# Gathers issued before scatters in each pass of an expert-choice feed-forward layer, on one Trainium2 core

## What is computed

```
def ffn(x, gate_w, w_gate, w_up, w_down):
    affinity = softmax(einsum('bsd,ed->bse', x, gate_w)).transpose(0, 2, 1)
    gating, idx = top_k(affinity, 256)              # each of 8 experts takes 256 of 1024 tokens
    x_in = x[bidx, idx]                             # gather
    h = silu(x_in @ w_gate[e].T) * (x_in @ w_up[e].T)
    x_e = h @ w_down[e].T
    return zeros_like(x).at[bidx, idx].add(gating[..., None] * x_e)   # scatter with add

x = x + 0.5 * ffn(layernorm(x), ...)
x = x + attention(layernorm(x), ...)                # 16 heads of 8, rotary in three dimensions
x = x + 0.5 * ffn(layernorm(x), ...)
```

## Time and profile before

| | us |
|---|---|
| three runs | 1326.4, 1331.73, 1332.17 (median 1331.73) |
| profiled execution, its own time | 1333.52 |
| its span, first to last instruction | 1331.7 |
| PE busy | 1122.5 (84%) |
| DVE busy | 1044.5 (78%) |
| ACT busy | 768.2 (58%) |
| POOL busy | 448.9 (34%) |

### The profile page before, as it was taken

The page is one execution under the profiler, slowest core; times in us unless marked ns, Lnnn a source line. Parts: engine busy times, 40 slices in busy tenths (PEclk is TensorE's granted clock), DMA queues, the critical chain, the costliest instruction groups (busy, mean ns, idle before and its releaser), DMA issues.

```text
span 1331.7 us, 25142 instructions
## 1 busy us (share of the span) xinstructions
PE 1122.5 (84%) x9424; PEld 476.4 (36%) x9424; DVE 1044.5 (78%) x2182; ACT 768.2 (58%) x1433; POOL 448.9 (34%) x431
## 2 busy tenths in 40 slices
PE   3159898999487999999899998899978889889884
PEld 3126565666131222222222222122313256556553
DVE  3676966764986999999999999899896685975531
ACT  2043112532246999999789996889778843121120
POOL 3034777688256111100000000004000025777674
PEclk9999999999587999999999998999999988999887
DMA  8023446456612311112201131101220224444442
GB/s 264 6 56 68 82 86 141 82 128 139 174 43 80 87 31 38 43 43 52 63 17 31 41 82 48 40 8 41 73 57 4 56 58 95 100 87 85 104 89 20
DMA packets 92122, 94.54 MB, mean 71 GB/s; under 512 B 14464, under 2 KB 68992, under 8 KB 91968
## 3 DMA queue, kind: packets, MB, share of 16 engines
q1 hardware_dynamic: 69472, 76.13, 20.5%
q0 software_dynamic: 22528, 16.79, 9.6%
HBM read 63.12 MB, written 31.59 MB: 71 GB/s over the span
## 4 chain that ended last, share of the span: by engine, by line
DVE 50%; PE 25%; POOL 8%; issue 7%; ACT 5%; DMA 3%; DVEq 0%; POOLq 0%; ACTq 0%
DVE mx L1549 34%; PE pA L1072 4%; PE pS L1061 4%; DVE ge L1275 4%; POOL out_dram L553 3%; PE pO L1185 3%; PE pO L1062 2%; DMA xg<-zd,idx 2%; DVE onehot L1362 2%; POOL x L553 2%; ACT Pt L893 2%; DVE scr L1434 2%; PE pS L1206 2%; POOL xg L535 2%; PE pS L1062 1%
## 5 line engine op out<-in xcount | busy, mean ns | idle before, releaser
L1549 DVE TENSOR_REDUCE mx<-pA 128x2 f32<-128x1024 f32 x512 | 589.3, 1216 | 26.8 <-PE pA L1117 25.3
L893 ACT ACTIVATE Pt<-pS 128x512 f32<-128x512 f32 x1024 | 556.2, 596 | 75.7 <-PE pS L1206 70.3
L1185 PE MATMUL pO<-Pt,Vst 128*16 128x256 f32 x4096 | 327.9, 393 | 11.5 <-ACT U L884 11.5
L793 ACT ACTIVATE Pt<-pS 128x512 f32<-128x512 f32 x128 | 76.3, 597 | 245.6 <-PE pS L1061 245.4
L595 POOL TENSOR_TENSOR mparts<-mx,onesm 128x32 bf16<-128x32 f32 x16 | 4.0, 252 | 518.0 <-DVE mx L1554 511.3
L1117 PE MATMUL pA<-Kst,Qst 48*128 48x512 bf16 x704 | 144.3, 406 | 36.6 <-DVE mx L1549 34.8
L535 POOL DMA_INDIRECT xg<-zd,idx x128 | 125.7, 982 | 142.0 <-issue 73.1
L1061 PE MATMUL pS<-Pt,wg 128*128 128x512 f32 x256 | 147.6, 660 | 14.5 <-DVE Pt L1394 9.4
L1206 PE MATMUL pS<-Qst,Kst 51*128 51x512 bf16 x704 | 141.5, 398 | 10.7 <-ACT Pt L893 5.1
L1185 PEld LDWEIGHTS pO<-Pt,Vst 128*16 128x16 f32 x4096 | 68.3, 94 | 206.5 <-issue 116.7
L1072 PEld LDWEIGHTS pA<-wd,Pt 128*128 128x128 f32 x1024 | 120.9, 192 | 20.3 <-issue 15.0
(11 more groups left out here) (170 smaller groups left out, 1140.0 us busy)
## 6 DMA issues: line engine op xcount, KB each, us to landing
wg<-w_gate_dram SPq DMA_DIRECT2D x32, 256.0 KB, 2.8
wu<-w_up_dram SPq DMA_DIRECT2D x32, 256.0 KB, 3.1
wd<-w_down_dram SPq DMA_DIRECT2D x32, 256.0 KB, 3.9
qk<-parts SPq DMA_DIRECT2D x64, 96.0 KB, 2.7
Kst<-qk SPq DMA_DIRECT2D x132, 32.0 KB
zd<-Z SPq DMA_DIRECT2D x8, 512.0 KB, 4.1
vp<-pair SPq DMA_DIRECT2D x4, 1024.0 KB, 5.3
Vst<-vp SPq DMA_DIRECT2D x16, 256.0 KB
```

Source lines behind the costliest of these rows:

```text
L893: S.activation(Pt[:, s % 4, j, r * 512:(r + 1) * 512], pS[:, bank_of(k, 4 * s + 2 * j + r), :], ACT.Exp, scale=SCALE).then_inc(s_exp, 1)
L1185: last = M.matmul(pO[32 * h:32 * h + 16, cols], Vst[k][:, s % 8, h, :], Pt[:, s % 4, h // 2, (h % 2) * 512 + 256 * a:(h % 2) * 512 + 256 * ...
L1549: V.reduce_max(mx2[:, k, 2 * j:2 * j + 2, c, half], pA[ring[q, a] % 2][:, :, :], AX.X).then_inc(s_Ar, 1)
```

## The change

Three things change; all sums stay the same apart from the order in which three parts of a factor are added.

1. POOL's order in a pass: `gather(it + 2)` stands ahead of `scatter(it - 1)`, in both FFNs, except in pass 22.
2. The `rest` and `lowest` of parts 0 and 1 move from POOL to DVE (passes 12 to 14); those of parts 2 and 3 stay on POOL, after `scatter(15)`. `middle(2)` on ACT moves from pass 15 to behind it. On SP, `load(0)` and `load(1)` move ahead of `load_weights(16)`, and `store_parts(2)` behind the reload of X.
3. `expert_values`, which copied one expert's slots and factors, is gone; `onehots` and `compact` read them in place. `pick` reads PSUM in place with two reductions, where it copied to `picked` and added three times. Its waits and the four buffers of `idx` stay.

```diff
             for it in range(RUN):
-                if 13 <= it:
-                    lowest(it - 13)
-                if it in (12, 13):
-                    rest(it - 12)
+                if it + 2 < RUN:
+                    gather(it + 2)
                 if it:
                     scatter(it - 1)
-                if it + 2 < RUN:
-                    gather(it + 2)
                 if it == 2:
                     gains(1)
-                if it in (14, 15):
-                    rest(it - 12)
             scatter(RUN - 1)
+            rest(2)
+            rest(3)
+            lowest(2)
             lowest(3)
...
             for it in range(RUN, NIT):
+
+                if it + 2 < NIT and it != 22:
+                    gather(it + 2)
                 if it > RUN:
                     scatter(it - 1)
-                if it + 2 < NIT:
+                if it == 22:
                     gather(it + 2)
...
-            def expert_values(j):
-                hh = j // E
-                dve.wait_ge(s_vals, 6 * (hh + 1))
-                V.tensor_copy(slotE[:, :], slotT[hh % 2][:, :, j % E])
-                link(V.tensor_copy(valsE[:, :, :], vals[hh % 2][:, :, j % E, :]))
...
-                    last = V.tensor_scalar(onehot[:, b, c, :], slots[:, :], slotE[:, c * HB + b:c * HB + b + 1], None, ALU.is_equal)
+                    last = V.tensor_scalar(onehot[:, b, c, :], slots[:, :], slotT[j // E % 2][:, c * HB + b, e:e + 1], None,
+                                           ALU.is_equal)
...
-                link(V.tensor_copy(picked[r][:, :, :], pI[:, 0:5 * HB * SH].rearrange("p (k f) -> p k f", f=5)))
-                V.tensor_tensor(idx[r][:, :], picked[r][:, :, 0], picked[r][:, :, 1], ALU.add).then_inc(s_idx, 1)
+                picked = pI[:, 0:5 * HB * SH].rearrange("p (k f) -> p k f", f=5)
+                V.reduce_sum(gain[r][:, :], picked[:, :, 2:5], AX.X)
+                V.reduce_sum(row[:, :], picked[:, :, 0:2], AX.X).then_inc(s_row, 1)
+                dve.wait_ge(s_row, j + 1)
+                V.tensor_copy(idx[r][:, :], row[:, :]).then_inc(s_idx, 1)
...
-                link(V.tensor_tensor(gsum[:, :], picked[r][:, :, 2], picked[r][:, :, 3], ALU.add))
-                link(V.tensor_tensor(gain[r][:, :], gsum[:, :], picked[r][:, :, 4], ALU.add))
...
+                if (it, k) == (12, 1):
+                    rest(0)
+                if (it, k) == (12, 3):
+                    lowest(0)
+                if (it, k) == (13, 2):
+                    rest(1)
+                if (it, k) == (14, 0):
+                    lowest(1)
```

More of the change, by code:

```diff
@@ L160, in program @@
         res = [sb(f"res{i}", [P, CH, ROWS_H], F32) for i in range(2)]
-        slotE = sb("slotE", [P, HT], F32)
-        valsE = sb("valsE", [P, HT, 5], BF16)
         onehot = sb("onehot", [P, HB, CH, CAP], BF16)
-        picked = [sb(f"picked{i}", [P, HB * SH, 5], F32) for i in range(4)]
-        gsum = sb("gsum", [P, HB * SH], F32)
+        row = sb("row", [P, HB * SH], F32)
         idx = [sb(f"idx{i}", [P, HB * SH], I32) for i in range(4)]
@@ L247, in program @@
         s_comp = sem("comp")
+        s_row = sem("row")
         s_idx = sem("idx")
@@ L468, in _ @@
             store_parts(1)
+            load(0)
+            load(1)
+            store_values(1)
             load_weights(16)
-            load(0)
             load_weights(17)
-            store_parts(2)
-            store_values(1)
             for b in range(2, B):
@@ L476, in _ @@
                 load_x(b, x1_in)
+            store_parts(2)
             store_parts(3)
-            load(1)
             store_values(2)
@@ L770, in between @@
                     middle(1)
-                if (it, k) == (15, 0):
-                    middle(2)
                 if (it, k) == (16, 1):
@@ L815, in _ @@
                 expert(it)
+            middle(2)
             middle(3)
@@ L1036, in compact @@
                     pe.wait_ge(s_idx, j)
+                if j % E == 0:
+                    pe.wait_ge(s_vals, 6 * (j // E + 1))
                 for b in range(HB):
@@ L1371, in pick @@
                         dve.wait_ge(s_scat[b], adds_before(j - 4) + 32)
-                link(V.tensor_copy(picked[r][:, :, :], pI[:, 0:5 * HB * SH].rearrange("p (k f) -> p k f", f=5)))
-                V.tensor_tensor(idx[r][:, :], picked[r][:, :, 0], picked[r][:, :, 1], ALU.add).then_inc(s_idx, 1)
+                picked = pI[:, 0:5 * HB * SH].rearrange("p (k f) -> p k f", f=5)
[3 more added lines that the diff above has]
+                V.tensor_copy(idx[r][:, :], row[:, :]).then_inc(s_idx, 1)
                 if j >= NIT - E:
-                    V.scalar_tensor_tensor(idxo[r][:, :], picked[r][:, :, 0], float(HB * N), picked[r][:, :, 1], ALU.add, ALU.add)
-                link(V.tensor_tensor(gsum[:, :], picked[r][:, :, 2], picked[r][:, :, 3], ALU.add))
-                link(V.tensor_tensor(gain[r][:, :], gsum[:, :], picked[r][:, :, 4], ALU.add))
+                    V.tensor_scalar(idxo[r][:, :], row[:, :], float(HB * N), None, ALU.add)
             def outputs(j):
@@ L1420, in setup, with rest, lowest @@
                     add_products(u)
+            def rest(u):
+                dve.wait_ge(s_hi, u + 1)
+                V.tensor_tensor(scr[:, 2 + u % 2, :], scr[:, u % 2, :], parts[:, u % 2, 0, :], ALU.subtract).then_inc(s_rest, 1)
+            def lowest(u):
+                dve.wait_ge(s_mid, u + 1)
+                V.tensor_tensor(parts[:, u % 2, 2, :], scr[:, 2 + u % 2, :], parts[:, u % 2, 1, :], ALU.subtract).then_inc(s_parts, 1)
             def add_products(u):
@@ L1485, in expert @@
                 if not first and it + 2 < end and it + 2 not in (8, 24):
-                    onehots(3)
+                    onehots(it + 2, 3)
                 hidden(it, 1)
@@ L1493, in expert @@
                     if quarters:
-                        expert_values(it + 3)
-                        onehots(0)
+                        onehots(it + 3, 0)
                 between(it, 2)
@@ L1500, in expert @@
                 if quarters and it != 22:
-                    onehots(1)
+                    onehots(it + 3, 1)
                 between(it, 3)
@@ L1507, in expert @@
                     pick(24)
-                    expert_values(25)
-                    onehots(0)
-                    onehots(1)
+                    onehots(25, 0)
+                    onehots(25, 1)
                 if quarters:
-                    onehots(2)
+                    onehots(it + 3, 2)
                 between(it, 4)
             def all_onehots(j):
-                expert_values(j)
                 for quarter in range(4):
-                    onehots(quarter)
+                    onehots(j, quarter)
             def first_experts(j):
```

6 lines of the change are left out of this document (3 added, 3 removed).

## The result

The changed kernel took 1364.62 us (median of 4 runs, 1363.81 to 1365.63) beside 1330.16 us for the kernel before on the same chip (median of 4 runs, 1326.4 to 1332.17): ratio 1.0263, 95% interval 1.0236 to 1.0290. It is **slower** by 2.6%. The forecast was 1332.3 us in a range of 1316 to 1347, so the result lies 17.6 us above the range. The profiled run took 1365.63 us, its span is 1363.8 us, 32.1 us above the span before.

A forecast was written before the change was run, and what follows sets the result against it. It took PE's 24.5 us of waits for gathers queued behind scatters as the bound in plain passes. First FFN +1.3 and second -0.7 gave +0.6 us on a median of 1331.7: 1332.3 us, range 1316 to 1347.

The forecast's parts named there:

- -2.3: First FFN: with `rest` off POOL's passes, the last `pick` step is no longer slowed (2.20 us instead of 0.17): -2.3 us.
- Issue to landing 3.4 us: Plain passes: time from a scatter's issue to its landing, which `pick` waits for, taken as 3.4 us.
- the loop of 15.5 us: Plain passes: gather issues, scatter issues, landing, `pick`, next gather form a closed loop, 15.5 us a pass against 14.1 before.
- The bounds: Loop period: 15.0 us with minimum issues and a 3.2 us landing, 16.5 us with gathers near their longest.
- one with norms and projections its own 15.9: First FFN, experts 6 to 15: one of nine passes takes its own 15.9 us, the other eight 15.5 us.
- the sentence on SP: SP's queue: moving `load(0)` ahead of a weight load and `store_parts(2)` behind the reload of X costs 0.
- -1.8: First FFN: ACT no longer sits 4.72 us in pass 15 for `rest(2)`; with a smaller gap in pass 14, -1.8 us.
- -1.0: First FFN, experts 4 to 6: search passes that DVE fills gain what DVE saves, -1.0 us.
- -1.3: Before either FFN: reading slots and factors in place shortens DVE's three one-hot groups and two picks, -1.3 us each.
- Pass 30 can then begin 1.0 us later ...: 0: Second FFN's end: pass 30 starts 2.8 us late, but its transpose no longer waits 2.87 us, so it costs 0.
- The stall lowers the clock where there is no room: Rival: PE also stops in passes 9 to 13 and 18 to 22, then runs at the lower clock: 1345 us; 20%.
- The loop does not close: Rival: scatters land early enough for every `pick`, so most transpose waits for gathers vanish: 1304 us; 10%.

The follow-up runs named there:

- late loads: Changed kernel, weight loads also wait for the scatter landing that `pick` awaits: 1360.4 us, ratio 1.022; without this for experts 14, 15, 24, 30, 31: 1356.7 us, 1.009.
- waits per batch alone: Changed kernel with four buffers, each scatter's issues waiting only for earlier adds to their own batch: 1357.8 us, ratio 1.009 to the kernel before.

## Why the prediction was wrong

*That a loop closes* through the four `idx` buffers was right, with the wait where it was said to be, and so was the list of its pieces. The sizes were wrong. The prediction's terms and what the two traces show, in us of difference to the kernel before:

| stretch | predicted | measured |
|---|---|---|
| first FFN, `idx` of expert 6 to 15 | +7.7 | +21.1 |
| first FFN, the rest, to the first reduction of the attention | -6.4 | -2.8 |
| attention, to `idx` of expert 16 | 0 | +3.8 |
| second FFN, `idx` of expert 16 to 25 | -1.7 | +4.4 |
| second FFN, `idx` of expert 25 to 31 | +5.8 | +9.0 |
| last `idx` to the end | -4.8 | -3.3 |
| sum | +0.6 | +32.1 |

The predicted terms are those of its sum: -6.4 is -2.3 - 1.0 - 1.3 - 1.8, -1.7 is 1.6 - 1.0 - 1.3 - 1.0, and -4.8 is the +1.0 for an end to which the last `pick` comes 5.8 us late.

- **"Issue to landing 3.4 us", the loop of 15.5 us.** This is the mis-sized term. The median over all issues is 3.4 in both kernels, but the loop waits for the last of four, and in the changed kernel that one often meets the weight loads: 3.8 to 6.2 us. Measured: 16.1 to 17.7 us between the gathers of experts 6 to 12, 16.0 on the mean from 25 to 31, and 18.2 from `idx` 19 to 20, where the landing took 6.20. With the loads out of the way it was 15.4 to 15.5 in plain passes. The bounds went to 16.5 with longer gathers (four at 1.325 us make it nearer to 17), and held no longer landing, though the earlier trace rows had one of 7.4 us. Nine passes of the first FFN took 153.3 us where 139.9 was said; with late loads the gathers of experts 6 and 15 are 146.3 us apart, so about half of the miss there is the landing.
- **"Passes 10 to 13 keep 15.3 to 16", "one with norms and projections its own 15.9".** This shows in the other half: with late loads the gathers of experts 9 to 15 are still 15.8 to 17.8 us apart. The reload of X waits for scatter 7, and expert 10's weights are queued behind it on SP; the sentence on SP weighed the two moved lines and not who is queued behind a wait for a scatter that itself moves. From the transpose of pass 9 to that of pass 10 are 21.9 us, 14.4 before.
- **"-2.3", "-1.8", "-1.0", "-1.3"** in the first FFN, 6.4 us of savings outside these nine passes: 2.8 came. With the low parts alone 1.8 of 4.1 came. Why the rest did not is not shown.
- **"Pass 30 can then begin 1.0 us later ...: 0", and +1 for the lower clock.** This let a last `pick` 5.8 us late cost 1 us at the end, by TensorE's chain. The end is the queue of scatters behind the last gather, and it gave back 3.3 us of the 13.4 by which the last `idx` lags beyond the 22.0 that were there at the start of the second FFN. This is a small term.

Two slips in the working changed little. The last scatter issue 5.75 us after the first does not follow from issues of 1.56 us with 0.3 between (5.6; measured 5.69). And a pair of 1.02 us is not in the earlier trace rows, which have 1.10, though elsewhere in the trace most pairs take 1.02.

*The attention*, said to keep its length within 1 us, was 3.8 us longer, in both traces of the changed kernel (731.8 and 731.6). In the traces of the other 18 runs it lies between 725.3 and 732.3 us, and not by the parts of the change (726.5 with waits per batch alone, 732.3 with the old order), so the difference is not explained and no cause is claimed.

*The rivals.* "The stall lowers the clock where there is no room" had the right sign and its sum (1345) was nearer, but most of its mechanism was not what came. Granted clock and work of four stretches of the changed kernel (us, PE busy, PEld, DVE, ACT, POOL, clock, share of DMA, GB/s):

```profile
222.30:239.10 16.80, 13.70 (x86) 8.39 (x84) 7.23 (x27) 2.98 (x5) 9.95 (x8) 0.90 0.33 61
...
277.40:292.60 15.20, 15.20 (x100) 9.88 (x98) 10.29 (x29) 5.66 (x11) 9.86 (x8) 1.00 0.43 79
292.60:308.90 16.30, 15.52 (x100) 9.97 (x99) 11.05 (x29) 4.71 (x10) 11.33 (x8) 1.00 0.40 78
1246.40:1263.50 17.10, 13.68 (x86) 8.45 (x85) 7.34 (x28) 2.98 (x5) 10.87 (x9) 0.90 0.38 80
```

It spoke of passes 9 to 13 and 18 to 22. In passes 11 to 13 the clock is 1.00. It is lower from 239.10 to 261.04 (0.84, before 0.88) and from 1137.26 to 1157.40 (0.78, before 0.92), so two of its passes bear it out; but passes 18 to 22 together take 83.0 us where they took 83.5. Most of the lower clock is 0.90 in plain passes, behind TensorE's waits for the loop. The one-hots did not shut the gathers out: with six buffers the same one-hots run beside gathers at 12.7 us a pass. "The loop does not close" is what five or six buffers make of the kernel; for it the prediction said 1304 us on a chip of 1331.7, and the six buffers gave a ratio of 0.984, some 1309.

*The named signs* came in part. `pick` waits for scatters, but 3.5 us on the mean and up to 5.2, where 1 to 3 was said. Gather starts in the plain passes were not 15.4 to 15.6 us apart, and passes 10 to 13 did not keep their length. One transpose besides the two first ones still waited, 5.08 us in pass 23. "16.5 or more would mean that a scatter's landing or the clock was mis-sized" is what came in six of the nine steps from expert 6 to 15; from 25 to 31 they were 15.5 to 16.4 us.

## What to carry to other kernels

When an order is turned round on a queue, follow each buffer of each step that moves back to the one who writes it next, and count the distance in passes: here four buffers of 16 bytes per partition and one order made a loop from GpSimd over the DMA and VectorE back to GpSimd, and a fifth buffer turned the loss into a gain of 1.8%. A loop's period is summed from the instance it waits for (the last issue of the pass, with what is transferred beside it then), not from medians over all. And find the end of the kernel on the queue that ends last before a delay upstream is costed at nothing.

## What the runs showed that was not expected

- A scatter of 128 rows mostly lands 3.2 to 3.3 us after the start of its issue when nothing is loaded beside it (at the most 3.9 us, and once 4.63), and 3.8 to 6.2 us with the first load of an expert's 768 KB of weights issued within 2 us of it.
- A scatter's issue is longer beside a VectorE step with two operands in SBUF: 2.50 us in place of 1.56 for this one of pass 13, beside the `lowest` that the change moved there (timeline of the changed kernel). Three gathers beside such steps took 1.56, 1.83 and 1.84 us in place of some 1.0.

```profile
319.95 1.22 DVE L1423 TENSOR_TENSOR parts<-scr,parts 128x1024 bf16<-128x1024 f32 x1
320.11 2.50 POOL L551 DMA_INDIRECT x<-Pt,idx  x1 [0.30 <-issue]
```

- The kernel before takes 1327 to 1330 us on some chips and 1343 to 1351 on others, and the changed kernel 1365 and 1366 on one of either kind, so the same change measures 1.026 or 1.013.
